# SSM stage: smaller calls in a new order on four engines, and transposes that write in reading order

## What is computed

```python
zxbcdt = jnp.einsum('bld,ed->ble', u, W_in)          # z (256), x, B, C (512), dt (4)
dt = jax.nn.softplus(dt + dt_bias)
conv = conv_b
for w in range(D_CONV):                              # 4 taps along the tokens
    conv = conv + xp[:, w:w + L, :] * conv_w[:, w]
xBC = jax.nn.silu(conv)
...
def step(h, inp):                                    # a scan over the 512 tokens
    dA_t, dtx_t, B_t, C_t = inp
    h = h * dA_t[:, :, None, None] + jnp.einsum('bhp,bn->bhpn', dtx_t, B_t)
    y_t = jnp.einsum('bhpn,bn->bhp', h, C_t)
    return (h, y_t)
...
y = jnp.moveaxis(y, 0, 1) + x * D[None, None, :, None]
g = y * jax.nn.silu(z)
g = g * jax.lax.rsqrt(jnp.mean(g * g, axis=-1, keepdims=True) + EPS) * norm_w
return jnp.einsum('ble,de->bld', g, W_out)
```

## Time and profile before

| | us |
|---|---|
| median of 3 runs (lowest to highest) | 870.03 (869.9 to 875.33) |
| the profiled execution | 871.93 |
| its span, first to last instruction | 870.2 |
| busy PE, DVE, ACT, POOL | 770.9, 688.4, 553.1, 274.9 |
| first `states(0)` to last, 7 rows of the SSM stage | 378.3 to 641.9 |

### The profile page before, as it was taken

The page is one execution under the profiler, slowest core; times in us unless marked ns, Lnnn a source line. Parts: engine busy times, 40 slices in busy tenths (PEclk is TensorE's granted clock), DMA queues, the critical chain, the costliest instruction groups (busy, mean ns, idle before and its releaser), DMA issues.

```text
span 870.2 us, 14840 instructions
## 1 busy us (share of the span) xinstructions
PE 770.9 (89%) x3896; PEld 617.5 (71%) x3896; DVE 688.4 (79%) x1612; ACT 553.1 (64%) x934; POOL 274.9 (32%) x417
## 2 busy tenths in 40 slices
PE   6879998789999999787888879798886899999998
PEld 3657677667888887565767768576765678888886
DVE  3478888879999998576858778787756978999996
ACT  4555665778888887536355463645524878888885
POOL 2135443601111020043445463554544600111110
PEclk9999999889999999999999999999997999999999
DMA  8000000645555552000000000000003446565552
GB/s 232 2 1 3 5 2 20 214 145 189 181 192 180 191 180 96 1 0 1 1 2 1 3 3 1 3 0 2 0 2 104 159 168 207 190 199 193 193 195 77
DMA packets 29202, 76.95 MB, mean 88 GB/s; under 512 B 4867, under 2 KB 9438, under 8 KB 29150
## 3 DMA queue, kind: packets, MB, share of 16 engines
q1 hardware_dynamic: 28996, 76.36, 26.3%
q10 hardware_dynamic: 154, 0.00, 0.0%
HBM read 73.73 MB, written 2.62 MB: 88 GB/s over the span
## 4 chain that ended last, share of the span: by engine, by line
PE 52%; DVE 17%; issue 15%; POOL 7%; ACT 6%; DMA 1%; DVEq 0%; SPq 0%; POOLq 0%; ACTq 0%
PE ps L1493 6%; PE ps L1494 6%; PE ps L1474 6%; PE ps L1495 6%; PE ps L1475 6%; PE ps L1476 6%; POOL rt_small L399 4%; DVE conv_acc L1144 3%; PE ps L1646 3%; DVE gram L1199 2%; PE ps L1329 1%; DVE xn L1089 1%; DVE s_lo L1070 1%; DVE t L942 1%; PE ps L1523 1%
## 5 line engine op out<-in xcount | busy, mean ns | idle before, releaser
L715 ACT ACTIVATE s_ring<-ps,b1T 128x512 f32<-128x512 f32 x256 | 172.9, 689 | 72.1 <-PE ps L1495 71.2
L1104 DVE SCALAR_TENSOR_TENSOR s_ring<-s_ring,top_col,r_all 128x1024 f32<-128x1024 f32 x128 | 178.0, 1390 | 38.5 <-ACT s_ring L715 33.9
L1070 DVE TENSOR_TENSOR s_lo<-s_ring,s_hi 128x1024 fp32r<-128x1024 f32 x128 | 161.6, 1262 | 0.0
L703 ACT ACTIVATE s_hi<-s_ring 128x1024 fp32r<-128x1024 f32 x128 | 134.5, 1051 | 2.7 <-DVE s_ring L1104 2.7
L1493 PE MATMUL ps<-ffn_hi,w_hi 128*128 (+1 forms) x256 | 105.2, 411 | 1.0 <-issue 1.0
L1474 PE MATMUL ps<-s_hi,w_hi 128*128 128x512 f32 x256 | 102.3, 400 | 1.4 <-DVE s_lo L1070 1.4
L1494 PE MATMUL ps<-ffn_lo,w_hi 128*128 (+1 forms) x256 | 102.8, 401 | 0.0
L1495 PE MATMUL ps<-ffn_hi,w_lo 128*128 (+1 forms) x256 | 102.7, 401 | 0.0
L1475 PE MATMUL ps<-s_lo,w_hi 128*128 128x512 f32 x256 | 102.0, 398 | 0.0
L1476 PE MATMUL ps<-s_hi,w_lo 128*128 128x512 f32 x256 | 101.6, 397 | 0.0
L451 POOL CAST rows_r<-rows_f 80x512 fp32r<-80x512 f32 x16 | 17.8, 1109 | 259.3 <-DMA rows_f<-route_dram 259.3
(11 more groups left out here) (238 smaller groups left out, 1664.3 us busy)
## 6 DMA issues: line engine op xcount, KB each, us to landing
r_all<-route_dram SPq DMA_DIRECT2D x128, 512.0 KB, 4.3
out_dram<-X SPq DMA_DIRECT2D x8, 256.0 KB, 4.1
X<-in_L_attn_a_x_dram SPq DMA_DIRECT2D x1, 1792.0 KB, 10.0
rows_f<-route_dram SPq DMA_DIRECT2D x48, 32.0 KB, 2.6
w_rows<-in_L_ffn_mlp_w_dram SPq DMA_DIRECT2D x1, 1024.0 KB, 13.2
route_dram<-route_cols SPq DMA_DIRECT2D x64, 8.0 KB, 1.4
in_rows<-in_L_attn_b_W_in_dram SPq DMA_DIRECT2D x1, 384.0 KB
X<-in_L_attn_a_x_dram SPq DMA_DIRECT2D x1, 256.0 KB, 2.8
```

The source lines that it names most:

```text
L703: eng.activation(s_hi[:, q % NR, :, :], s_ring[:, q % NR, :, :], ACT.Copy).then_inc(F["hi"], 1)
L715: eng.activation(s_ring[:, q % NR, e % 2, :], bank(e % 4), ACT.Silu, bias=b1T[:, e:e + 1], scale=ALPHA).then_inc(F["act"], 1)
L1070: eng.tensor_tensor(s_lo[:, q % NR, :, :], s_ring[:, q % NR, :, :], s_hi[:, q % NR, :, :].bitcast(F32), ALU.subtract).then_inc(F["lo"], 1)
L1104: eng.scalar_tensor_tensor(out=s_ring[:, q % NR, :, :], in0=s_ring[:, q % NR, :, :], scalar=top_col[:, 0:1], in1=r_all[:, q % NR, :, :], o ...
```

## The change

Three things are done.

Transposes: `xn_turn`, `u_turn` and `g_turn` write their columns with a stride into PSUM, so that the bank holds reading order (for g the reverse, block by block). The copies of ACT and DVE behind the first two are then straight, and `out_proj` reads straight weights.

Calls: `front` becomes `cb_of`, `xb_turn` and `seg_sum`; `back` becomes `y_skip`, `y_state`, `y_gram` and `next_state`; each half of `conv` and each quarter of `z_proj` is a call; `conv_taps_of` becomes single `conv_tap`s; the masking `cb_out` is taken out of `grams`, and `fade` out of `weigh`.

Order: `step` is written anew on PE, DVE, ACT and POOL. No arithmetic is added or left out.

```diff
-            gT = own("gT", [P, 2, SEQ])
+            gT = own("gT", [P, 2, NT, SEQ // NT])
...
                 wait(eng, S1["xnT_ps"], b + 1)
...
-                eng.activation(xnT[:, par, :].rearrange("d (p r) -> d r p", r=NT),
-                               bank(4).rearrange("d (r p) -> d r p", r=NT), ACT.Copy).then_inc(S1["xnT"], 1)
+                eng.activation(xnT[:, par, :], bank(4), ACT.Copy).then_inc(S1["xnT"], 1)
...
-                    mm = eng.transpose(bank(7)[:, r * P:(r + 1) * P], xn[:, r, :], ident[:, :])
+                    mm = eng.transpose(bank(7)[:, r:SEQ:NT], xn[:, r, :], ident[:, :])
...
-                    mm = eng.transpose(bank(5)[:, j * P:(j + 1) * P], gn[:, c % 2, j * P:(j + 1) * P], ident[:, :])
+                    mm = eng.transpose(bank(5)[:, j * P:(j + 1) * P].rearrange("e (r p) -> e p r", r=NT),
+                                       gn[:, c % 2, j * P:(j + 1) * P], ident[:, :])
...
-                        mm = eng.matmul(bank(at)[:, r * D:(r + 1) * D], gT[:, j, r:SEQ:NT], outT[:, j, :], start=(j == 0),
+                        mm = eng.matmul(bank(at)[:, r * D:(r + 1) * D], gT[:, j, r, :], outT[:, j, :], start=(j == 0),
...
+            def cb_out(b, c):
+                n = NT * b + c
+                wait(eng, M["cb_ps"], n + 1)
+                wait(eng, M["gram"], NH * (n - 1))
+                eng.tensor_tensor(cb[:, c % 2, :], bank(0)[:, 0:P], upto[:, :], ALU.mult).then_inc(M["cb"], 1)
...
+            def fade(b, par, c):
+                wait(eng, M["state"], (NT - 1) * b + c)
...
                 if second:
-                    states(i, 0)
-                    ys(i, odd, 0)
-                if first:
-                    conv_taps_of(i + 1, 0)
-                    conv_taps_of(i + 1, 1)
...
+                    ys(i, odd, 2)
+                    states(i, 2)
+                    norms(i, 1)
+                if first:
+                    softplus(i + 1, 1 - odd)
+                if second:
+                    ys(i, odd, 3)
+                    norms(i, 2)
```

More of the change, by code:

```diff
@@ L534, in step @@
                 if second:
[L535 to L538, removed]
+                    rms(i, 2)
                 if first:
@@ L541, in step @@
                 if second:
-                    rms(i, 2)
-                if third:
-                    router_chain(R2, i - 1)
+                    gate(i, odd, 3)
                 if first:
@@ L1242, in step @@
                     ssm_stats(i + 1)
+                if fourth:
+                    router_norm(R2, i - 2)
                 if second:
-                    grams(i, odd, 0)
+                    cb_out(i, 0)
                 if third:
@@ L1256, in step @@
                     u_low(i + 1)
+                if third:
+                    router_stats(R2, i - 1, M["x"])
                 if second:
+                    cb_out(i, 2)
+                    ys(i, odd, 0)
                     states(i, 0)
-                    ys(i, odd, 0)
+                    grams(i, odd, 2)
                 if first:
-                    conv_taps_of(i + 1, 0)
-                    conv_taps_of(i + 1, 1)
-                if second:
-                    norms(i, 0)
-                if first:
-                    dt_arg(i + 1)
-                if second:
-                    states(i, 1)
-                    ys(i, odd, 1)
+                    conv_tap(i + 1, 0, 1)
                 if fourth:
@@ L1272, in step @@
                 if second:
-                    grams(i, odd, 2)
+                    cb_out(i, 3)
+                if first:
+                    conv_tap(i + 1, 0, 2)
+                if fourth:
+                    router_top(R2, i - 2)
+                if first:
+                    conv_tap(i + 1, 0, 3)
+                    dt_arg(i + 1)
+                    conv_tap(i + 1, 1, 1)
+                if second:
+                    ys(i, odd, 1)
+                    states(i, 1)
+                if first:
+                    conv_tap(i + 1, 1, 2)
+                if second:
+                    grams(i, odd, 3)
+                    norms(i, 0)
+                if first:
+                    conv_tap(i + 1, 1, 3)
+                if second:
+                    ys(i, odd, 2)
+                    states(i, 2)
+                    norms(i, 1)
                 if first:
@@ L1655, in step @@
                 if second:
-                    front(i, odd, 0)
-                    front(i, odd, 1)
+                    seg_sum(i, 0)
+                    cb_of(i, odd, 0)
+                    xb_turn(i, odd, 0)
+                    y_skip(i, odd, 0)
+                    cb_of(i, odd, 1)
                 if third:
                     g_turn(i - 1, 3)
-                if first:
-                    u_turn(i + 1)
+                if second:
+                    seg_sum(i, 1)
                 if third:
```

257 lines of the change are left out of this document (144 added, 113 removed).

## The result

The changed kernel takes **825.4 us** (median of 4 runs, 823.0 to 825.74), the kernel before 870.44 beside it (869.9 to 875.33): a ratio of 0.9465 [0.9426, 0.9503], 5.4% faster. The profiled execution took 825.74 us, its span is 824.0. The forecast was 821, range 805 to 848.

What follows compares the result with a forecast made beforehand. Order and waits bounded the kernel before; DVE was to bound SSM rows at 32.0 us. Seven distances −42, tail −5, first row's chain −1, attention −1.5 took 871.93 to 822.4; less 1.9 for the median, 821 us, range 805 to 848.

Steps and rivals of the forecast that it cites:

- The straight copies and out_proj: SSM row: straight copies win ACT 0.51 us and DVE 0.38; out_proj takes 1.8 us, PE wins 1.95.
- The strided transposes as free: PE's transposes in SSM and attention still start 0.125 us apart when writing PSUM with a stride; nothing taken.
- both rivals on them: Strided transposes cost 2.1 times (830 us) or 4 times (855), chance 0.09; at 7 times, slower, 904 us, chance 0.03.
- The waits: DVE's five waits in an SSM row, 6.47 us together, all have cover in the new order and go.
- `u_low` is due at 11.65: this is the tightest place, 0.4 us: DVE's walked SSM row: ACT's copy ends near 11.2, leaving 0.4 us, which slow transposes would open.
- And 0.4 for waits that my walk missed: Allowance of 0.4 us in the SSM row's forecast of 32.0 us.
- the rival: SSM rows: waits move instead of going, half of the 6.47 us stays, the clock included; 845 us, chance 0.22.
- gaps of 1 to 2 us ahead of `cb_of(1)`: Expected sign in PE's SSM row: idle 1 to 2 us there and ahead of next_state(1).
- DVE becomes the bound: SSM row: DVE's work without waits, 31.2 − 0.38 = 30.8 us, sets the row; 806 to 834 us, chance 0.62.
- The term beside POOL: SSM row: DVE steps slow beside POOL's two-input operations; 17% more of them meet work, 0.8 us.
- The tail: End of the SSM stage, 29.2 us before: forecast 24 us, range 21 to 27, so −5.
- at most 8 × 0.33 = 2.6: −1.5: Attention: PE, the full engine, waited 0.33 us a row for the copy; 1.5 us won.

Runs made afterwards that it cites:

- The two halves: Kernel before with only the transposes, straight copies and straight out_proj weights: 856.8 us; changed kernel without these, so new calls and order only: 840.9 us.
- norms_first: Changed kernel with norms(3) and cb_out(0) ahead of router_norm in DVE's order: 820.2 us, ratio 0.941 to the kernel before.
- norms_act: Changed kernel with all four norms moved from DVE to ACT and cb_out(0) ahead of router_norm: 816.9 us, ratio 0.9364 to the kernel before.
- warm_gap: Changed kernel with ten unused products a row in PE's gap between y_skip(0) and cb_of(1): 819.7 us, ratio 0.9421 to the kernel before.

## Why the prediction was right, and where it was not

**The straight copies and out_proj**: right. 0.62 for `xnT_out`, 0.60 for `u_out`, 0.68 for `u_low`, 1.78 us from the start of `out_proj` to the next at full clock, for 1.8. The two halves show what it is worth together with `u_low` and `u_out`: 1.3 to 1.5 us a loop row in the old order. But 1.95 holds at full clock only. At half clock the straight product takes 3.40 and the strided one 3.73, and the row from which the prediction read the 3.73 was one of half clock.

**The strided transposes as free**: right, and so both rivals on them fell. A transpose of `u_turn` takes 274 ns on average (273 in the median, as before), one of `g_turn` 273 in the median, as before, and four of `u_turn` start within 0.43 us, 0.11 apart. The Trainium skill's sentence on non-contiguous access in PSUM (PSUM — Partial Sum Buffer, Specifications) did not show here for fp32 transposes whose columns step 16 or 128 bytes; the measurement decides.

**The waits**: the five named ones are gone or shrunk at full clock (no bracket over 0.3 in the row of 32.4). The sentence "`u_low` is due at 11.65: this is the tightest place, 0.4 us" was the right place. What opened it was not slow transposes but `out_proj` at half clock. So the step that failed is the term "And 0.4 for waits that my walk missed": it was 0 at full clock and 1.2 to 1.5 with the fallen one. The prediction put the clock under the rival and priced it at nothing, since the kernel before had rows of 0.95 and 1.00 of like length (without the branch 37.2 and 37.6 at 0.95, 37.5 at 1.00). They were of like length because in the two at 0.95 half clock lay under the strided `out_proj`, which takes 3.73 to 3.76 us at either clock. The change took this cover away: in three of five rows `out_proj` took 3.0 to 3.4 us and not 1.8. The gap ahead of it was forecast as "gaps of 1 to 2 us ahead of `cb_of(1)`" and taken as harmless. It was 2.3.

**DVE becomes the bound**: right for the loop rows (on norms_first, whose rows are of the same work: DVE operation +1.2 to 1.4 us a row, PE +0.2 or less at full clock). The first two rows PE bounds. The term beside POOL was mis-sized: 0.8 was forecast. DVE's busy time went from 29.5 to 31.0 although `u_low` lost 0.38: 1.9 us. The share of idle time that vanished was no measure of it. Which operations come to lie beside POOL's decides, as for the first four `gram` of a row, 2.27 in place of 1.13; in the row of 32.4 the sixteen `gram` make up 1.5 of the 1.9 (6.05 us for 4.55). With 1.9 for 0.8 and without the 0.4, the sum is 30.8 + 1.9 = 32.7, for 32.4 measured.

**The sum**: the first two rows took 28.1 each, not 30 (−3.7). There the chain of states was named as the limit, and it is PE, busy but for 0.3 and 0.5 us: unused products on it lengthened these rows, as shown above. The other five took 168.2 and not 161.5 (+6.7). Against 32.0 these are 1.9 and 1.7 more in the two at 0.95, 5.8 more with the branch (1.5 were forecast for it), 0.4 more in the one at full clock and 1.7 less in the last, which lacks part of the router's work. **The tail** gained 6.4 for 5. That 825.4 comes so near 821 is in part luck: −3.7 and +6.7 have different causes, and so have the −1.4 of the tail and the +1.8 of a stage without a change.

**Attention**: the term "at most 8 × 0.33 = 2.6: −1.5" failed. The wait of 0.33 is gone, and four rows take 61.38 us, where they took 61.41: PE waits for `probs` in its place (0.59 us in one of them). The 1.0 us that is won ahead of the SSM stage was there before attention's first copy (9.4 against 10.6 us): PE's first instruction waited 5.73 us for a DMA, where it had waited 6.92.

**What stays open**: the second expert layer, 1.8 us longer without a change in it (the kernels here spread over 3.6 us there); what decides whether a gap of PE of 2.3 us is followed by half clock, and why it also fell behind the dt products; and why the branch cost 0.3 in norms_act.

## What to carry to other kernels

When a reordering makes one engine the bound, look at what its partners now do in their idle time. A stretch in which PE idles or runs only small products can be free in the sum and still be followed by half clock for the work behind it. A product whose strided weights make it as slow at full clock as at half hides such a fall; make it faster and the fall starts to cost. Work on POOL that nobody waits for can lengthen DVE's operations without any bracket. Split a block on the bounding engine where another engine waits for its first result, and price the reordering and the copies apart: here they added up. And compare variants by the rows that the edit touches: here most of the 5 us between the medians of warm_gap and the changed kernel came from elsewhere.

## What the runs showed of the hardware

- Behind a PE gap of 2.3 us the granted clock read 1.00 for another 1.4 us and then 0.51 for 3.4 us (changed kernel, second loop row); with 2.4 us of unused products in the gap it stayed at 1.00 there. It also fell behind small products with no gap (warm_gap, at 500).
- `out_proj` with strided weights took 3.73 us at clock 0.50 and at 1.00, with straight ones 3.40 and 1.78.
- An operation on POOL of 1.09 us lengthened DVE's `gram`s by 0.79 us. A tap, one of whose inputs is in PSUM, took 0.73 us beside `xw` (changed kernel, at 471.15) and 0.74 with POOL idle (at 472.10).
- fp32 transposes into PSUM with a step of 16 or 128 bytes: 273 ns in the median, as straight ones.
- DVE's bracket at the loop's backward branch: 2.7 to 3.2 us in eleven kernels, 0.46 in the two whose list on DVE is four operations a row shorter.
